# Low halves of Wsoma and Wtemp on GpSimd, and Wtemp's transposes moved from TensorE to VectorE

## The reference, cut to what matters

```python
ctx = causal_ema(x, tau_ctx)
wg = sigmoid(concat([x, ctx]) @ Wg.T + bg)
gated = x * wg
h1 = gelu(x @ Wn1.T + bn1)
mod = 0.5 + sigmoid(h1 @ Wn2.T + bn2)                  # 2 numbers for each token
traces = [causal_ema(gated * mod[d], tau[d]) for d in range(2)]
temporal = sum_d(traces[d] * softmax(blend)[d])
gate = sigmoid(temporal @ Wtemp.T + btemp)
soma = gelu(x @ Wsoma.T + bsoma)
x = x + layernorm((soma * gate) @ Wout.T)
```

## Time and profile before

| | before |
|---|---|
| median of 3 runs | 721.21 us |
| lowest, highest | 720.27, 721.3 us |
| profiled execution | 721.11 us |
| its span, first to last instruction | 719.3 us |
| busy TensorE, VectorE | 713.5, 547.1 us |
| busy ScalarE, GpSimd | 372.2, 140.8 us |

### The profile page before, as it was taken

One profiled execution on the slowest core, in us unless ns is written; L12 is line 12 of the kernel. 1 busy time (PEld: TensorE's weight loads), 2 busy tenths in 40 slices (PEclk: granted clock), 3 DMA queues, 4 the chain that ended last, 5 costly groups with the idle time before them and its releaser, 6 DMA issues.

```text
span 719.3 us, 10000 instructions
## 1 busy us (share of the span) xinstructions
PE 713.5 (99%) x3261; PEld 588.5 (82%) x3261; DVE 547.1 (76%) x824; ACT 372.2 (52%) x554; POOL 140.8 (20%) x256
## 2 busy tenths in 40 slices
PE   9999999999999999999999999999999999999998
PEld 8877888888888888888888888888888888888886
DVE  5799796695596587579569569987888887897583
ACT  4365446435535545544644553564756574664530
POOL 2000030022004004004003103313262242123210
PEclk9999999999999999999999999999999999999999
DMA  7959307934953970990891582657155658353312
GB/s 220 264 108 181 63 1 107 197 78 80 194 107 58 175 146 16 177 183 3 134 183 62 97 213 100 165 160 248 65 146 184 183 132 182 103 134 103 88 73 88
DMA packets 141871, 93.55 MB, mean 130 GB/s; under 512 B 108703, under 2 KB 124094, under 8 KB 140046
## 3 DMA queue, kind: packets, MB, share of 16 engines
q1 hardware_dynamic: 139310, 86.56, 52.8%
q10 hardware_dynamic: 1184, 4.23, 1.7%
q0 software_dynamic: 1344, 2.36, 1.3%
HBM read 32.28 MB, written 25.20 MB: 80 GB/s over the span
## 4 chain that ended last, share of the span: by engine, by line
PE 94%; DVE 4%; issue 1%; ACT 1%; POOL 0%; ACTq 0%; DVEq 0%; POOLq 0%
PE pc L728 12%; PE pc L730 12%; PE pc L729 12%; PE pt L728 8%; PE pt L730 8%; PE pt L729 8%; PE pm L728 4%; PE pm L730 4%; PE pm L729 4%; PE pm L854 4%; PE pm L856 4%; PE pm L855 4%; PE pm L735 3%; PE pm L980 1%; PE pm L978 1%; PE pm L979 1%
## 5 line engine op out<-in xcount | busy, mean ns | idle before, releaser
L728 PE MATMUL pc<-x_h,wg_h 128*128 128x512 f32 x224 | 87.7, 391 | 0.1
L730 PE MATMUL pc<-x_h,wg_l 128*128 128x512 f32 x224 | 87.3, 390 | 0.0
L729 PE MATMUL pc<-x_l,wg_h 128*128 128x512 f32 x224 | 87.3, 390 | 0.0
L1585 DVE TENSOR_TENSOR_SCAN stage_b<-alpha,carry,stage_b 128x512 f32<-128x512 f32 x64 | 78.5, 1269 | 0.0
L1226 ACT ACTIVATE ctx_t<-ctx_t,col_all 128x512 f32<-128x512 f32 x32 | 23.1, 723 | 54.3 <-DVE ctx_t L1565 54.3
L728 PEld LDWEIGHTS pc<-x_h,wg_h 128*128 128x128 f32 x224 | 42.1, 188 | 10.6 <-issue 1.9
L854 PE MATMUL pm<-t_h,wt_h 128*128 128x512 f32 x128 | 50.1, 392 | 0.6 <-DVE t_l L1598 0.6
L855 PE MATMUL pm<-t_l,wt_h 128*128 128x512 f32 x128 | 49.9, 390 | 0.0
L856 PE MATMUL pm<-t_h,wt_l 128*128 128x512 f32 x128 | 49.9, 389 | 0.0
L730 PE MATMUL pm<-wo_h,s_l 128*128 128x512 f32 x128 | 49.8, 389 | 0.0
L728 PE MATMUL pm<-wo_h,s_h 128*128 128x512 f32 x128 | 49.8, 389 | 0.0
(11 more groups left out here) (264 smaller groups left out, 1952.7 us busy)
## 6 DMA issues: line engine op xcount, KB each, us to landing
x_planes<-x_pairs SPq DMA_DIRECT2D x56, 256.0 KB, 7.0
xt_scratch<-x_t SPq DMA_DIRECT2D x8, 1024.0 KB, 10.0
n_scratch<-stage_a SPq DMA_DIRECT2D x8, 1024.0 KB, 9.6
ctx_t<-xt_scratch SPq DMA_DIRECT2D x16, 512.0 KB, 6.2
out_dram<-x_tok SPq DMA_DIRECT2D x28, 256.0 KB, 2.3
x_pairs<-n_scratch SPq DMA_DIRECT2D x10, 512.0 KB, 5.3
mod<-mod_scratch ACTq DMA_DIRECT2D x8, 512.0 KB, 3.7
x_planes<-stage_b SPq DMA_DIRECT2D x60, 64.0 KB, 2.3
```

The lines of the kernel that those rows point to most:

```text
L728: nc.tensor.matmul(acc, ah, bh, start=start and q == 0, stop=False)
L729: nc.tensor.matmul(acc, ah, bl, start=False, stop=False)
L730: last = nc.tensor.matmul(acc, al, bh, start=False, stop=stop and q == n - 1)
L1585: nc.vector.tensor_tensor_scan(tr[:, m % 2, :], alpha[:, 1 + d:2 + d].to_broadcast([P, BLK]), tr[:, m % 2, :], carry[:, D - d, m:m + 1], A ...
```

## The change

Three things change, all of them in the prologue.

1. Wtemp lands as squares, as Wsoma does (`load_squares`, four DMAs instead of one), and both are turned in place in SBUF by VectorE (`turn_raw`). TensorE's 16 transposes of Wtemp go. The high halves are read from SBUF instead of PSUM.
2. The eight low halves of Wsoma and Wtemp are made by GpSimd (`weight_lo`), behind `carry_context(0)` and in front of the first `carry_traces`. TensorE waits for them on `w_lo_pool`, and so does `weave_wout`.
3. ScalarE and VectorE get new orders around them: ScalarE makes Wsoma's four high halves ahead of the first `z_tanh` and Wtemp's behind the second and the third; VectorE has Wtemp's turns behind `gate_x(0, 0)` and `modulate(0, 0)`.

```diff
-            def load_soma():
-                squares = t["L0_cond_Wsoma"].rearrange("(b i) (k a f) -> a i k b f", i=32, a=4, f=32)
+            def load_squares(n):
+                src = t["L0_cond_Wsoma"] if n == WSOMA else t["L0_cond_Wtemp"]
+                raw = L0W[n][2]
+                squares = src.rearrange("(b i) (k a f) -> a i k b f", i=32, a=4, f=32)
+                if n == WTEMP:
+                    sp.wait_ge(w_turned, W_BEFORE[WGC] + 4)
                 for a in range(4):
...
-            load_soma()
+            load_squares(WSOMA)
             turn_x(1, x_spread, 0)
-            load_weight(WTEMP)
+            load_squares(WTEMP)
             store_xt(0)
             spread_x(1, x_woven, 0)
...
+            def weight_lo(n):
+                for k in range(W_COUNT[n]):
+                    hi, lo = w_dest(n, k)
+                    pool.wait_ge(w_hi, W_BEFORE[n] + k + 1)
+                    nc.gpsimd.tensor_tensor(lo, L0W[n][2][:, k, :], hi.bitcast(F32), ALU.subtract).then_inc(w_lo_pool, 1)
+
             def step(i, first=False, ends=False, last=False):
                 k = 0 if ends else 1
                 carry_context(i, k)
+                if first:
+                    weight_lo(WSOMA)
+                    weight_lo(WTEMP)
                 carry_traces(i, 0, k)
...
-                    if n != WSOMA:
+                    if n not in BY_SQUARES:
                         prepare(n, chunks)
             def ready(n):
                 pe.wait_ge(w_hi, W_BEFORE[n] + W_COUNT[n])
-                pe.wait_ge(w_lo, W_BEFORE[n] + W_COUNT[n])
+                if n in (WSOMA, WTEMP):
+                    pe.wait_ge(w_lo_pool, RAW_BEFORE[n] + W_COUNT[n])
+                else:
+                    pe.wait_ge(w_lo, W_BEFORE[n] + W_COUNT[n] if n < WSOMA else W_LO_COUNT + W_COUNT[n])
...
-                act.wait_ge(w_turned, W_TURNS_BEFORE[WTEMP] + 4)
+                act.wait_ge(w_lo_pool, 8)
                 act.wait_ge(wout_spread, 64)
...
-            for m in range(NC):
-                z_tanh(0, m)
-                prepare_behind(BEHIND_V, m)
+            prepare_behind(BEHIND_V, 0)
+            prepare_behind(BEHIND_V, 1)
+            z_tanh(0, 0)
+            z_tanh(0, 1)
+            prepare_behind(BEHIND_V, 2)
+            z_tanh(0, 2)
+            prepare_behind(BEHIND_V, 3)
+            z_tanh(0, 3)
...
-            def turn_soma(chunks):
+            def turn_raw(n, chunks):
+                raw = L0W[n][2]
                 for k in chunks:
-                    c = W_BEFORE[WSOMA] + k
-                    dve.wait_ge(weight_in[WSOMA], 16 * 4)
-                    dve.wait_ge(w_hi, c - 3)
-                    dve.wait_ge(w_lo, c - 3)
-                    nc.vector.transpose(w_bank(WSOMA, c).rearrange("p (b i) -> p b i", i=32),
-                                        soma[:, k, :].rearrange("p (b f) -> p b f", f=32)).then_inc(soma_turned, 1)
+                    dve.wait_ge(weight_in[n], 16 * 4)
+                    nc.vector.transpose(raw[:, k, :].rearrange("p (b i) -> p b i", i=32),
+                                        raw[:, k, :].rearrange("p (b f) -> p b f", f=32)).then_inc(raw_turned, 1)
...
+            turn_raw(WSOMA, (0, 1))
+            scan_context(0, 3)
+            turn_raw(WSOMA, (2, 3))
             gate_sum(0, 0)
-            prepare_behind(BEHIND_V, 0)
             gate_sum(0, 1)
             gate_x(0, 0)
-            prepare_behind(BEHIND_V, 1)
+            turn_raw(WTEMP, (0, 1))
             gate_sum(0, 2)
             gate_x(0, 1)
             modulate(0, 0)
-            prepare_behind(BEHIND_V, 2)
+            turn_raw(WTEMP, (2, 3))
             gate_sum(0, 3)
             gate_x(0, 2)
             scan_traces(0, 0)
-            prepare_behind(BEHIND_V, 3)
             gate_x(0, 3)
```

More of the change, by code:

```diff
@@ L142, in residual_chain_kernel @@
         w_turned, w_hi, w_lo = sem("w_turned"), sem("w_hi"), sem("w_lo")
-        soma_turned = sem("soma_turned")
+        raw_turned, w_lo_pool = sem("raw_turned"), sem("w_lo_pool")
         tx_done, h1_mm, u_mm, v_mm, mod_mm, soma_mm, wt_mm, wo_mm = (
@@ L265, in residual_chain_kernel @@
         W_BEFORE = [sum(W_COUNT[:n]) for n in range(6)]
-        W_TURNS_BEFORE = [sum(W_COUNT[m] for m in range(n) if m != 3) for n in range(6)]
+        BY_SQUARES = (WSOMA, WTEMP)
+        RAW_BEFORE = {n: 4 * q for q, n in enumerate(BY_SQUARES)}
+        W_LO_COUNT = sum(W_COUNT[:WSOMA])
         BEHIND_U = [[(WGC, [2, 3])], [(WGX, [0, 1])], [(WGX, [2, 3])], []]
@@ L325, in load_weight @@
                 _, src, raw = L0W[n]
+                sp.dma_start(raw[:, :, :], src).then_inc(weight_in[n], 16)
+            def load_squares(n):
+                src = t["L0_cond_Wsoma"] if n == WSOMA else t["L0_cond_Wtemp"]
+                raw = L0W[n][2]
+                squares = src.rearrange("(b i) (k a f) -> a i k b f", i=32, a=4, f=32)
                 if n == WTEMP:
                     sp.wait_ge(w_turned, W_BEFORE[WGC] + 4)
-                sp.dma_start(raw[:, :, :], src).then_inc(weight_in[n], 16)
-            def load_soma():
-                squares = t["L0_cond_Wsoma"].rearrange("(b i) (k a f) -> a i k b f", i=32, a=4, f=32)
                 for a in range(4):
-                    sp.dma_start(soma[32 * a:32 * a + 32, :, :].rearrange("i k (b f) -> i k b f", f=32),
-                                 squares[a]).then_inc(weight_in[WSOMA], 16)
+                    sp.dma_start(raw[32 * a:32 * a + 32, :, :].rearrange("i k (b f) -> i k b f", f=32),
+                                 squares[a]).then_inc(weight_in[n], 16)
             def load_x(i, j):
@@ L1120, in prepare @@
                     hi, _ = w_dest(n, k)
-                    if n == WSOMA:
-                        act.wait_ge(soma_turned, k + 1)
-                    else:
-                        act.wait_ge(w_turned, W_TURNS_BEFORE[n] + k + 1)
-                    nc.scalar.activation(hi, w_bank(n, c), ACT.Identity, scale=W_SCALE[n]).then_inc(w_hi, 1)
+                    if n in BY_SQUARES:
+                        act.wait_ge(raw_turned, RAW_BEFORE[n] + k + 1)
+                        src = L0W[n][2][:, k, :]
+                    else:
+                        act.wait_ge(w_turned, W_BEFORE[n] + k + 1)
+                        src = w_bank(n, c)
+                    nc.scalar.activation(hi, src, ACT.Identity, scale=W_SCALE[n]).then_inc(w_hi, 1)
             def prepare_behind(lists, m):
@@ L1489, in prepare @@
                     dve.wait_ge(w_hi, c + 1)
-                    nc.vector.scalar_tensor_tensor(lo, w_bank(n, c), W_SCALE[n], f32(hi), ALU.mult,
+                    src = L0W[n][2][:, k, :] if n in BY_SQUARES else w_bank(n, c)
+                    nc.vector.scalar_tensor_tensor(lo, src, W_SCALE[n], f32(hi), ALU.mult,
                                                    ALU.subtract).then_inc(w_lo, 1)
@@ L1721, in _ @@
             nc.vector.tensor_tensor(wn2_l[:, :], col_wn2[:, :], f32(wn2_h[:, :]), ALU.subtract).then_inc(consts_v, 1)
-            for c in range(NC):
-                scan_context(0, c)
-                prepare_behind(BEHIND_U, c)
-                if c == 2:
-                    turn_soma((0, 1))
-            turn_soma((2, 3))
+            scan_context(0, 0)
+            prepare_behind(BEHIND_U, 0)
+            scan_context(0, 1)
+            prepare_behind(BEHIND_U, 1)
+            scan_context(0, 2)
+            prepare_behind(BEHIND_U, 2)
+            turn_raw(WSOMA, (0, 1))
+            scan_context(0, 3)
+            turn_raw(WSOMA, (2, 3))
             gate_sum(0, 0)
-            prepare_behind(BEHIND_V, 0)
             gate_sum(0, 1)
             gate_x(0, 0)
-            prepare_behind(BEHIND_V, 1)
+            turn_raw(WTEMP, (0, 1))
             gate_sum(0, 2)
```

## The result

The changed kernel took 725.05 us (median of 16 runs, 723.72 to 734.98), the kernel before 721.94 beside it (16 runs, 720.27 to 726.11): ratio 1.005, 95% interval 1.0025 to 1.0074. It is slower by 3.1 us. (The ratio leaves out the longest run of the changed kernel, which lies over 1.5% above its shortest.) Forecast were 722.5 us, 1.3 later, and a range up to 725.0: the sign is right, the size is not, and the median lies just outside. The profiled execution took 724.69 us, its span is 722.9, against 721.11 and 719.3 before.

What follows compares the result with a forecast made beforehand. TensorE bounds the kernel, through when its matmul at 54.43 starts. VectorE gains 2.4 us, collisions cost 3.25: 0.8 later, or 2.0 with the tie lost; 1.3 taken, 721.2 + 1.3 = 722.5 us, range 718.9 to 725.0.

Steps and rivals of the forecast that it cites:

- One number decides: The start of the temporal matmul at 54.43 us on TensorE: every microsecond earlier or later should reach the kernel's end.
- VectorE's walk without collision, 2.4 us gained: VectorE's instruction order in the prologue: gate_x(0,3) at 42.8 instead of 45.17, and all that follows 2.4 us earlier.
- rival 4: GpSimd's subtractions slower than 1.29 us: at 1.6, four holds each 0.3 longer, 1.2 us more, 723.7; chance 8%.
- (a): On VectorE, gate_x(0,1) at 36.06 meets the first Wtemp subtraction: 0.46 us later.
- (b): The second Wtemp subtraction waits for gate_x(0,1), then holds VectorE's first modulate(0,0) to 38.3: 1.04 us later.
- (c): The third Wtemp subtraction, 40.9 to 42.2, holds VectorE's gate_x(0,2), due at 41.3: 0.75 us later.
- (d): The fourth Wtemp subtraction waits for gate_x(0,2), then holds VectorE's first scan to 43.9: 1.0 us later.
- The tie: gate_x(0,0) at 33.35 against the fourth Wsoma subtraction at 33.40: if GpSimd is first, VectorE waits 1.25 us more.
- The clock: TensorE's wait of some 2.8 us at 48.9 might lower its granted clock; 0.5 us of the range's upper end.
- The squares land from 34 on: Wtemp's four DMAs land between 33.9 and 38.1, taken as 34; each microsecond beyond 34.2 delays the chain by one.
- SP's queue moved by 4.5 us: Store_xt(0), spread_x(1) and Wout's transpose move back some 4.5 us; the spread may land up to 45.5 at no cost.
- rival 2: The collisions of VectorE and GpSimd don't happen: 2.4 us earlier, 718.8, or 719.9 with one left; chance 22%.

Runs made afterwards that it cites:

- F: The changed kernel with Wtemp fetched by one plain DMA and GpSimd filling zeros instead of subtracting the eight low halves: 718.77 us, 2.6 below the kernel before.
- K: Half the change: Wsoma turned in place with low halves on GpSimd, gate_x(0,0) ahead of gate_sum(0,1), Wtemp as in the kernel before: 720.01 us, 1.3 below it.
- H: The changed kernel with Wtemp's low halves back on VectorE, gate_x(0,0) first, Wtemp's squares issued earlier, temporal_hi(0,0) ahead of the weaves: 724.28 us, 3.0 above the kernel before.
- B: The changed kernel with GpSimd filling the eight low halves with zeros instead of subtracting: 721.37 us, 0.1 above the kernel before.
- A: The changed kernel with 16 more matmuls in TensorE's wait before the first temporal product: 723.73 us, 2.5 above the kernel before.
- C: The changed kernel with gate_x(0,0) ahead of gate_sum(0,1) on VectorE: 725.36 us, 4.1 above the kernel before.
- D: The changed kernel with all eight low halves of Wsoma and Wtemp back on VectorE: 722.96 us, 1.7 above the kernel before.
- E: The changed kernel with Wtemp fetched by one plain DMA instead of four DMAs of squares, subtractions kept: 724.58 us, 3.3 above the kernel before.
- I: H with ScalarE's order of the changed kernel and Wtemp's squares issued by GpSimd on its own queue: 722.33 us, 1.0 above the kernel before.
- G: The changed kernel with Wtemp's squares ahead of the transpose of x on SP's queue: 724.85 us, 3.5 above the kernel before.
- J: H with ScalarE's order of the changed kernel and Wtemp fetched by one plain DMA: 719.69 us, 1.7 below the kernel before.

## Why the prediction was right and wrong

- *One number decides.* Right for the changed kernel, F and K: the first is 3.1 us late at 60 us and 3.1 in the median, and F and K end earlier by about what they gain there (F 2.9 and 2.6, K 1.4 and 1.3). It isn't a rule: H was 1.4 us ahead at 60 us and lost it, and 1.3 more, between 75 and 111 us.
- *VectorE's walk without collision, 2.4 us gained.* Right: F gained 2.6 in the median. From `gate_sum(0,1)` to `gate_x(0,3)` the walk said 32.75 to 42.8; F has 32.27 to 42.28.
- *TensorE's part.* Right: Wsoma's products started at 38.17 for 38.0, and in F the temporal products at 48.32 for 48.9, where this execution ran about half a microsecond early (`gate_sum(0,1)` at 32.27 for 32.75).
- *GpSimd's part.* Right: unhindered subtractions took 1.28 to 1.30 us for 1.29, so rival 4 did not happen.
- *Two SBUF inputs wait for a subtraction, and the waiting GpSimd has the next turn.* Right, for the scan as well. The terms: (a) `gate_x(0,1)` 0.81 for 0.46, (b) `modulate` 1.03 for 1.04, (c) `gate_x(0,2)` 0.82 for 0.75, (d) scan 1.03 for 1.0 (durations of the changed kernel less those of B).
- *The tie.* This is the first step that failed. I put `gate_x(0,0)` at 33.35 against the fourth subtraction at 33.40 and took the middle between the two outcomes, a little down. `gate_sum(0,1)` started 0.26 later than forecast, GpSimd was first, and the hold was 1.07. The four terms together were 3.69 us for 3.25, mostly by (a), and with the 1.07 of the tie the holds sum to 4.76; less the 2.4 gained, 2.36 later, the measured 2.3 of `gate_x(0,3)`. The prediction's own case with the tie lost, 2.0, was short by 0.3. A tie should have been two cases with a time each, not a mean.
- *The clock.* The second step that failed. I left 0.5 us at the upper end of the range for a wait of 2.8, and nothing in the forecast; the wait was 4.0, and the fall cost 0.8 (A). The two levels of the granted clock bound it once it falls: ten matmuls at 0.43 instead of 0.23 are 2.0 us, less what the wait for the second `t_l` takes anyway. The forecast 0.5 us of waiting for the second `t_l` is gone, as the slow matmuls fill it. 2.3 and 0.8 make the 3.1 us that the profile is late at 60 us, and the medians differ by 3.1. Two small steps behind 450 us (0.3) and behind 690 us (0.15) bring this one execution to 3.6; I did not trace them.
- *The squares land from 34 on.* In the profiled execution VectorE didn't wait, since the holds had put its turn to 35.29. In others it did: 2.1 us in C, 5.1 in D. I treated the landing as one number, with 33.9 to 38.1 as its bounds; it varies from run to run, up to 40.2 in D, with the issuing of Wsoma's squares ahead of it (10.3 to 14.3 us) and of its own (6.3 to 9.7). I take that for most of the tail to 735: no run above 727.41 stands in E, F, I and K or among the other 11 of G and of H. J's 729.21 is an exception, and no long run of the changed kernel itself was profiled, so this stays argued.
- *SP's queue moved by 4.5 us, "at no cost up to 45.5".* The shift was too small: the squares took 6.3 to 9.7 us to issue, not 5.07, and the spread landed 5 to 7 us later (11 in D's long profile). In B, where it landed at 46.4, it did hold `temporal_hi`. It costs nothing in the median of the changed kernel, and 2.6 as soon as the rest works (B against F). I had priced each cover for the forecast alone; in rival 2, which I gave 718.8, this cover is gone, and B took 721.37. Without collisions the change as written would have been no gain.

## What to carry to other kernels

Work moved from VectorE to GpSimd isn't free beside VectorE instructions with two SBUF inputs: put each subtraction on the time axis beside them, let whatever meets one under way wait for its end (0.2 to 1.1 us here), let the next subtraction in before VectorE's next one, and work out both outcomes for a tie. Before you count a gain, price its cover again as if the gain were there: a queue that is late by 5 us may be hidden only by the loss you mean to remove. And take small pieces by DMA only where the queue behind them has room for their worst run: of this change, the half that needed no further squares gained when run alone, and with the other half the whole lost.

## What the runs showed of the hardware that I had not expected

- After a wait of 4 us of TensorE and 1.3 us of work at 1.00, the granted clock was 0.50 for 3.4 us; with G it was 0.50 for 6.8 us (51.35 to 58.17), already before the first matmul behind the wait, at 53.30. Over the changed kernel's 16 runs the mean granted clock sorts the times: 0.997 and 0.998 up to 725.12 us, 0.995 and less from 725.51. E has the same two groups without Wtemp's squares (up to 724.64, and from 725.44), so part of the spread is the clock's. With 16 filler matmuls in the wait it stayed at 1.00.
- How long a hold lasts can be read off: each `gate_x` and `modulate` that met a subtraction under way ended 0.54 to 0.56 us behind that subtraction's end, wherever in it they had met. In the changed kernel `gate_x(0,0)`, issued at 33.61, met one of 33.51 to 34.82 and ended at 35.36; in K, issued at 31.43, it met one that ended at 31.75 and ended at 32.30, so it was held for 0.2.
- A scan on VectorE is held by a subtraction of GpSimd (2.30 us in C, where its usual 1.28 stood in the kernel before), like other instructions with two SBUF inputs; a GpSimd fill of the same tile holds nothing.
- Four DMAs with 128-byte pieces, 1 MB together, keep SP's queue 10.3 to 14.3 us for Wsoma and 6.3 to 9.7 for Wtemp; GpSimd's queue issued the same in 4.57 us, and SP's, beside it, took 18.24.
- A store of 4 KB took 2.0 us from issue to landing 7.9 us behind a large spread on another queue, and 5.8 us 4.2 behind it (2.3 us at 7.5 behind in J, 2.5 at 7.3 in I). What else differed at that moment was not separated.
